# Down of a tile in parts behind up of the next, and late u and q activated by VectorE

## What is computed

```python
x_proj = silu(x @ W1 + b1);  u, v, q, k = split(x_proj, 4)       # 16 heads of 8
attn = silu(einsum('bqhd,bkhd->bhqk', qh, kh)) / S               # 16 x 2048 x 2048
av = einsum('bhqk,bkhd->bqhd', attn, vh)
y = layernorm(av * u, gamma, beta) @ W2 + b2
x = layernorm(x + y)
h = silu(fp4(x) @ fp4(w_gate).T) * (fp4(x) @ fp4(w_up).T)        # 352 wide
x = layernorm(x + fp4(h) @ fp4(w_down).T)
```

## Time and profile before

| | us |
|---|---|
| median of 3 runs | 516.2 |
| the profiled execution | 516.33 |
| its span, first to last instruction | 514.2 |
| first silu of the scores starts | 14.94 |
| last silu of the scores starts | 493.55 |
| TensorE busy | 496.7 (97%) |
| ScalarE busy | 487.3 (95%) |
| VectorE busy | 285.8 (56%) |
| POOL busy | 81.4 (16%) |
| 512 silus of the scores, busy | 474.8, mean 1182 ns for one |

### The profile page before, as it was taken

The page is one execution under the profiler, slowest core; times in us unless marked ns, Lnnn a source line. Parts: engine busy times, 40 slices in busy tenths (PEclk is TensorE's granted clock), DMA queues, the critical chain, the costliest instruction groups (busy, mean ns, idle before and its releaser), DMA issues.

```text
span 514.2 us, 20251 instructions
## 1 busy us (share of the span) xinstructions
PE 496.7 (97%) x9062; PEld 264.5 (51%) x9064; DVE 285.8 (56%) x730; ACT 487.3 (95%) x547; POOL 81.4 (16%) x180
## 2 busy tenths in 40 slices
PE   8899999999999999999999999999999999999996
PEld 5453335444344444434344444444477777777762
DVE  7644934655848375664847366573844433435445
ACT  4999999999999999999999999999999999999940
POOL 8413000102020200202020110202020202112010
PEclk9999999999999999999999999999999999999999
DMA  4732450000000000000000000000000000000000
GB/s 128 190 95 61 112 146 22 1 3 7 3 8 1 8 2 3 6 3 8 1 9 1 8 1 3 6 3 7 3 8 4 9 4 10 4 9 10 3 4 10
DMA packets 15173, 11.87 MB, mean 23 GB/s; under 512 B 1815, under 2 KB 14750, under 8 KB 15086
## 3 DMA queue, kind: packets, MB, share of 16 engines
q1 hardware_dynamic: 13800, 8.85, 6.5%
q0 software_dynamic: 704, 1.33, 0.9%
q10 hardware_dynamic: 582, 0.40, 0.3%
HBM read 1.92 MB, written 1.05 MB: 6 GB/s over the span
## 4 chain that ended last, share of the span: by engine, by line
ACT 51%; PE 28%; issue 17%; DVE 2%; DMA 1%; POOL 0%; POOLq 0%; SPq 0%; DVEq 0%
ACT attn L680 50%; PE ps L433 26%; PE ps L447 2%; DMA gate_b<-in_L_attn_b 1%; ACT feat L680 0%; ACT v_sb L680 0%; PE ps L467 0%; ACT uT L680 0%; POOL rstd_b L405 0%; DVE xn_b L817 0%; DVE stats_b L847 0%; DVE xn_b L825 0%; DVE xn_b L823 0%; DVE xn_b L821 0%; POOLq L136 0%
## 5 line engine op out<-in xcount | busy, mean ns | idle before, releaser
L680 ACT ACTIVATE attn<-ps 128x1024 f32<-128x1024 f32 x512 | 474.8, 1182 | 1.3 <-PE ps L433 0.8
L433 PE MATMUL ps<-attn,v_pad 128*32 128x256 f32 (+1 forms) x5120 | 274.4, 341 | 0.3 <-DVE wdown_t L1046 0.2
L433 PE MATMUL ps<-q_stack,k_stack 64*128 64x256 bf16 (+1 forms) x2560 | 172.9, 251 | 10.1 <-ACT attn L680 1.3
L433 PEld LDWEIGHTS ps<-attn,v_pad 128*32 128x32 f32 x5120 | 132.2, 109 | 80.3 <-issue 38.8
L433 PEld LDWEIGHTS ps<-q_stack,k_stack 64*128 64x128 bf16 x2560 | 79.0, 94 | 132.3 <-ACT attn L680 85.4
L404 POOL TENSOR_TENSOR ve_a<-mv_a,eps_col 128x1 f32<-128x1 f32 x24 | 4.6, 191 | 207.9 <-DVE mv_a L849 207.9
L404 POOL TENSOR_TENSOR ve_b<-mv_b,eps_col 128x1 f32<-128x1 f32 x24 | 4.6, 191 | 194.6 <-DVE mv_b L849 194.6
L433 PE MATMUL ps<-zeros 128*128 128x512 bf16 x49 | 13.9, 425 | 1.4 <-DVE zeros L973 1.2
L405 POOL TENSOR_TENSOR rstd_a<-ve_a,minus_half 128x1 f32<-128x1 f32 x24 | 13.5, 561 | 1.9
L405 POOL TENSOR_TENSOR rstd_b<-ve_b,minus_half 128x1 f32<-128x1 f32 x24 | 13.4, 560 | 1.9
L909 DVE COPY xqT<-ps 128x128 f32<-128x128 f32 x15 | 4.4, 292 | 16.2 <-PE ps L433 16.2
(11 more groups left out here) (189 smaller groups left out, 402.9 us busy)
## 6 DMA issues: line engine op xcount, KB each, us to landing
q_stack<-parts SPq DMA_DIRECT2D x18, 128.0 KB, 2.4
k_stack<-parts SPq DMA_DIRECT2D x12, 128.0 KB, 3.1
k_stack<-parts SPq DMA_DIRECT2D x15, 64.0 KB, 2.6
x_sb<-in_L_attn_x SPq DMA_DIRECT2D x3, 256.0 KB, 4.3
q_stack<-zeros SPq DMA_DIRECT2D x6, 128.0 KB, 2.5
k_stack<-parts POOLq DMA_DIRECT2D x9, 64.0 KB, 2.6
q_stack<-parts SPq DMA_DIRECT2D x8, 64.0 KB, 2.0
out<-x_a SPq DMA_DIRECT2D x8, 64.0 KB, 1.5
```

Source lines behind the costliest of these rows:

```text
L433: return pe.matmul(to, lhsT, rhs, start=start, stop=stop, skip_group_check=True)
L680: return act.activation(to, frm, ACT.Silu, **kw)
```

## The change

The kernel still computes the same. Three things are placed anew.

1. Down of tile t no longer is one job two steps behind its hqT. Its three products are issued behind up of tile t + 1: in three consecutive steps for wide tiles, the first two in one step and the third in the next for dense ones. up moves one step later in wide tiles. POOL makes x2 of tile t after x1 of tile t + 1.
2. u from token 512 on and q from token 1024 on are no longer projected in chunk 0. There are ten units of 256 tokens (`LATE`), one for each wide tile, projected in step +1 or +17 of the tile's chunk and activated by VectorE, in the way of `activate_gate` and in the buffers of the other tile: `late_read` at the unit's own job, `late_exponent` behind the copy of xqT, `late_sum` behind the copy of hqT, `late_product` (and a q's split) behind the next unit's `late_read`, or behind `late_sum` for the last.
3. The jobs of the weights come earlier, in steps 25, 27, 29 and 31 instead of 29, 31, 32 and 33. SP zeroes the rows of all q units first and copies the late parts in its loop over the tiles' outputs.

```diff
-               12: ("u", 0), 14: ("q", 256), 16: ("u", 1), 18: ("q", 512), 20: ("u", 2), 22: ("q", 1024),
-               24: ("u", 3), 26: ("q", 1536), 29: ("w2", 0), 31: ("gate", 0), 32: ("up", 0), 33: ("down", 0)}
+               12: ("u", 0), 14: ("q", 256), 18: ("q", 512), 25: ("w2", 0), 27: ("gate", 0), 29: ("up", 0),
+               31: ("down", 0)}
...
-    EVEN = {"y": 3, "xqT": 7, "gate": 8, "up": 10, "hqT": 16, "down": 18}
-    ODD = {"y": 19, "xqT": 23, "gate": 24, "up": 26, "hqT": 32, "down": 34}
+    EVEN = {"y": 3, "xqT": 7, "gate": 8, "up": 11, "hqT": 16}
+    ODD = {"y": 19, "xqT": 23, "gate": 24, "up": 27, "hqT": 32}
...
+    LATE = {0: ("q", 1024), 1: ("u", 512), 2: ("q", 1280), 3: ("u", 768), 4: ("q", 1536),
+            5: ("u", 1024), 6: ("q", 1792), 7: ("u", 1280), 8: ("u", 1536), 9: ("u", 1792)}
+    LW = 256
+    LATE_AT = {t: BEGIN[t // 2 + 1] + (17 if t % 2 else 1) for t in LATE}
+    PARTS_AT = {}
+    for t in range(1, DENSE + 1):
+        base, offsets = TILE_AT[t]
+        if t < WIDE:
+            first = base + offsets["up"] + 2
+            PARTS_AT |= {first: (t - 1, (0,)), first + 1: (t - 1, (1,)), first + 2: (t - 1, (2,))}
+        else:
+            first = base + offsets["up"] + 1
+            PARTS_AT |= {first: (t - 1, (0, 1)), first + 1: (t - 1, (2,))}
...
             for n in range(KT):
+                if n in LATE and LATE[n] in unit_no:
+                    stack(sp, unit_no[LATE[n]])
                 sp.wait_ge(x2_ready, n + 1)
...
+            def down_parts(at):
+                tile, parts = PARTS_AT[at]
+                k = job_no[("down", 0, tile)]
+                if at in FIRST_PARTS:
+                    wait_bank(at, k, JOB_BANK[k])
+                last = down_of(ROWS[tile % 2], JOB_BANK[k], 0, parts)
+                if at in JOB_AT:
+                    last.then_inc(job_made, 1)
...
+            def late_read(tile):
+                x, n, f, spare = late_buffers(tile)
+                col = 0 if LATE[tile][0] == "u" else 1
+                bank = wait_made("late", 0, tile)
+                dve.tensor_scalar(x, ps[:, bank, 0:LW], b1_col[:, col:col + 1], X_MIN,
+                                  ALU.add, ALU.max).then_inc(job_by_vec, 1)
+                wait_taken("late", 0, tile)
+
+            def late_exponent(tile):
+                x, n, f, spare = late_buffers(tile)
+                link(dve.tensor_scalar(n, x, -LOG2_E, Y_MIN, ALU.mult, ALU.max))
+                link(dve.tensor_scalar(spare, n, ROUND, None, ALU.add))
+                link(dve.scalar_tensor_tensor(out=f, in0=spare, scalar=ROUND, in1=n,
+                                              op0=ALU.subtract, op1=ALU.subtract))
+                link(dve.tensor_scalar(n.bitcast(U32), spare.bitcast(U32), 23, None, ALU.logical_shift_left))
+                link(dve.scalar_tensor_tensor(out=spare, in0=f, scalar=POWERS[4] / LAST, in1=f, op0=ALU.add, op1=ALU.mult))
+
+            def late_sum(tile):
+                x, n, f, spare = late_buffers(tile)
+                for power in (3, 2, 1):
+                    link(dve.scalar_tensor_tensor(out=spare, in0=spare, scalar=POWERS[power] / LAST, in1=f,
+                                                  op0=ALU.add, op1=ALU.mult))
+
+            def late_product(tile):
+                x, n, f, spare = late_buffers(tile)
+                kind, start = LATE[tile]
+                link(dve.scalar_tensor_tensor(out=spare, in0=spare, scalar=POWERS[0] / LAST, in1=n,
+                                              op0=ALU.add, op1=ALU.mult))
+                link(dve.tensor_scalar(spare, spare, LAST, 1.0, ALU.mult, ALU.add))
+                link(dve.reciprocal(f, spare))
+                link(dve.tensor_tensor(spare, x, f, ALU.mult))
+                if kind == "q":
+                    split(kind, start)
...
+                elif kind == "late":
+                    late_read(tile)
+                    if tile - 1 in LATE:
+                        late_product(tile - 1)
                 elif kind == "xqT":
                     copy_xqT(tile)
+                    if tile in LATE:
+                        late_exponent(tile)
...
                 elif kind == "hqT":
                     copy_hqT(tile)
+                    if tile in LATE:
+                        late_sum(tile)
+                        if tile + 1 not in LATE:
+                            late_product(tile)
```

More of the change, by code:

```diff
@@ L115, in build @@
         TILE_AT[t] = (BEGIN[WIDE // 2 + 1] + LAG + 1 + 12 * (t - WIDE),
-                      {"y": 0, "xqT": 4, "gate": 5, "up": 7, "hqT": 10, "down": 11})
+                      {"y": 0, "xqT": 4, "gate": 5, "up": 7, "hqT": 10})
     TILE_AT[DENSE] = (BEGIN[-2] + LAG, {"y": 1, "xqT": 5, "gate": 6, "up": 8, "hqT": 12})
+    LATE = {0: ("q", 1024), 1: ("u", 512), 2: ("q", 1280), 3: ("u", 768), 4: ("q", 1536),
[11 more added lines that the diff above has]
+            PARTS_AT |= {first: (t - 1, (0, 1)), first + 1: (t - 1, (2,))}
     JOB_AT = {at: (kind, i, None) for at, (kind, i) in PREP_AT.items()}
+    JOB_AT |= {at: ("late", 0, t) for t, at in LATE_AT.items()}
     for t, (base, offsets) in TILE_AT.items():
         JOB_AT |= {base + d: (kind, 0, t) for kind, d in offsets.items()}
+    JOB_AT |= {at: ("down", 0, t) for at, (t, parts) in PARTS_AT.items() if 2 in parts}
+    FIRST_PARTS = {at: t for at, (t, parts) in PARTS_AT.items() if 0 in parts}
     JOBS = [JOB_AT[at] for at in sorted(JOB_AT)]
@@ L318, in _ @@
                 zero_rows(sp, n)
-                stack(sp, n)
+            for start in (256, 512):
+                stack(sp, unit_no[("q", start)])
             for n in range(KT):
+                if n in LATE and LATE[n] in unit_no:
+                    stack(sp, unit_no[LATE[n]])
                 sp.wait_ge(x2_ready, n + 1)
@@ L411, in normalise, with make_x2 @@
                                           ALU.subtract, ALU.mult)
+            def make_x2(tile):
+                r = ROWS[tile % 2]
+                rstd(r, 2)
+                if tile >= 2:
+                    pool.wait_ge(out_written[tile % 2], 16 * (tile // 2))
+                normalise(r, r.x2[:, :], 2).then_inc(x2_ready, 1)
             for tile in range(TAIL - 1):
@@ L417, in _ @@
                 normalise(r, r.x1[:, :], 1).then_inc(x1_ready, 1)
[L418 to L421, removed]
+                if tile:
+                    make_x2(tile - 1)
             before = ROWS[(TAIL - 1) % 2]
@@ L562, in wait_spare, with wait_bank @@
                     pe.wait_ge(head_act, head_last[bank] + 1)
[L564 to L567, removed]
+            def wait_bank(at, k, bank):
                 if k:
@@ L574, in job @@
                     pe.wait_ge(av_taken, STEPS[at - LAG][0])
-                if tile is not None:
+            def down_parts(at):
[6 more added lines that the diff above has]
+                    last.then_inc(job_made, 1)
+            def job(at):
+                kind, i, tile = JOB_AT[at]
+                k = job_no[(kind, i, tile)]
+                bank = JOB_BANK[k]
+                wait_bank(at, k, bank)
+                if kind == "late":
+                    last = project(bank, *LATE[tile], LW)
+                elif tile is not None:
                     last = behind(kind, tile, bank)
@@ L612, in hqT_of, with down_of @@
                 return last
-            def down_of(r, small, off):
-                for t, (f0, fn) in enumerate(FT):
+            def down_of(r, small, off, parts=(0, 1, 2)):
+                for t in parts:
+                    fn = FT[t][1]
                     last = mm_rows(small, off, r.hqT[0:fn, t, :], wdown_t[0:fn, t, :], D, start=(t == 0), stop=(t == 2))
@@ L631, in behind @@
                     pe.wait_ge(hq_ready, tile + 1)
-                    return hqT_of(r, bank)
-                return down_of(r, bank, 0)
+                return hqT_of(r, bank)
             for at in range(len(STEPS)):
@@ L638, in _ @@
                     times_v(at - LAG)
[L639 removed]
+                if at in PARTS_AT:
+                    down_parts(at)
+                elif at in JOB_AT:
                     job(at)
@@ L779, in split @@
                     dve.wait_ge(head_act, head_no[(kind, start)] + 1)
-                else:
+                elif (kind, start) not in LATE.values():
                     dve.wait_ge(job_by_act, ACT_JOBS.index(job_no[(kind, start, None)]) + 1)
@@ L931, in activate_gate, with late_buffers @@
                 link(dve.reciprocal(f, spare))
+            def late_buffers(tile):
+                o = ROWS[(tile + 1) % 2]
+                kind, start = LATE[tile]
+                to = uT[:, start:start + LW] if kind == "u" else feat[:, unit_no[LATE[tile]] % FEAT, 0:LW]
+                return o.gate[:, 0:LW], o.magic[:, 0:LW], o.xn[:, 0:LW], to
+            def late_read(tile):
[20 more added lines that the diff above has]
+                x, n, f, spare = late_buffers(tile)
+                kind, start = LATE[tile]
```

(2 more changed lines are left out.)

7 lines of the change are left out of this document (4 added, 3 removed).

## The result

The changed kernel takes 518.75 us, the median of six runs (517.52 to 519.01), against 516.2: a ratio of 1.0046 with an interval of 1.0035 to 1.0057. It is slower, by 2.55 us; the forecast was 518.5. The profiled execution took 518.91 us, its span is 517.1. The times of most kernels here come in two groups up to 1.5 us apart, and in the traces this difference lies ahead of the first silu of the scores, which starts at 13.4 to 13.6 us in some and at 14.6 to 14.9 in the others. So I compare the traces from that silu on: it starts at 14.94 us before and at 14.86 after, and the last silu ends 2.93 us later behind it than before.

A forecast was written before the change was run, and what follows sets the result against it. ScalarE was taken as the bound, busy for all but half a microsecond from 80.80 to 494.90 us. Gains and losses summed to about +2.3 us on the profiled 516.33, or 518.5 from the median 516.2; range 515.4 to 520.8.

The forecast's parts named there:

- chunk 0, five activations: Chunk 0, steps 16 to 27: five 128x512 activations leave ScalarE at 0.57 us each, 2.86 us gained.
- steps 34 and 36: First chunk's end: the 0.19 us lost at step 34 goes, as the weights' gate, up and down no longer follow each other.
- dense stage, open before: Tiles 10 to 13: down and y crowding lost ScalarE 0.22 x 3 + 0.46 us; 1.1 us open to gain.
- dense stage, new: Dense tiles, steps 7 to 10: up, down's parts and hqT push TensorE's lag past 0.83; 0.13 lost five times, 0.66 us.
- four boundaries: Chunk boundaries, tiles 2, 4, 6, 8: y waits for zu behind late_product; 1.16 us lost each, 4.6 in four.
- odd tiles 1, 3, 5, 7: Product and q's split delay y and so xqT; with gate the lag is 1.05, 0.21 to 0.22 lost each, 0.84 us.
- tile 10: Step 192: late_sum and late_product of tile 9 follow hqT, so zu comes late; 0.42 us lost.
- The price of the product: late_product at 256 columns on VectorE: 3.04 us, its reciprocal 1.753 by the line through 22 and 352 columns.
- the free lag of 0.83: Score loop: TensorE may lag 0.83 us before ScalarE loses; scores must start 1.45 us before their first silu's due end.
- (a): Rival at the boundaries: product at most 2.2 us, zu reaches TensorE in time, boundary losses go; 512.8 us; chance 0.14.
- (b): Rival: VectorE's chain is 0.15 us shorter at each place, 0.3 less at each boundary; 516.4 to 517.2 us; chance 0.09.
- (c): Rival: VectorE's delays pile up; each boundary costs 1.7, each odd tile 0.5; +3.4 more, 521.9 us; chance 0.09.
- (d): Rival in chunk 0: TensorE's 512-column jobs feed ScalarE, so 2.86 us isn't gained; 521.4 us; chance 0.02.

The follow-up runs named there:

- experiment 2: Changed kernel with VectorE making zu ahead of late_product and a late q's split moved behind to_out of its tile: 511.76 us, ratio 0.9918.
- experiment 3: Changed kernel, own order, without the late silu's arithmetic (late_exponent, late_sum, four instructions of late_product); VectorE only copies the biased projection: 511.73 us, ratio 0.9924.
- Experiment 5: Changed kernel with one more 256-column tensor_tensor, its result unused, at the end of every late_product: 522.44 us, ratio 1.0126.
- experiment 1: Changed kernel with VectorE making zu of a finished chunk ahead of the odd tile's late_product: 512.14 us, ratio 0.9937.
- experiment 7: Changed kernel with down whole in its old steps and POOL's x2 in the old order, late silus kept: 545.96 us, ratio 1.0586.
- experiment 4: Kernel before the change with only down in parts at its new place and POOL's x2 a tile later, no late silus: 514.97 us, ratio 0.9984.

## Why the prediction was right

The mechanism forecast is the one that was found, and the time was right to 0.3 us. That is partly luck: two of its terms were off by 1.0 and by 0.66, in opposite directions, and the sum of the ends is 0.6 over the forecast, which the medians of the two kernels, 2.55 apart, don't show in full. In ScalarE's ends, between the kernel before and the changed one:

| term | forecast | measured |
|---|---|---|
| chunk 0, five activations | -2.86 | -2.71 |
| steps 34 and 36 | -0.19 | -0.28 |
| dense stage, open before | -1.1 | -1.13 |
| dense stage, new | +0.66 | 0 |
| four boundaries | +4.6 | +4.88 |
| odd tiles 1, 3, 5, 7 | +0.84 | +1.84 |
| tile 10 | +0.42 | +0.34 |
| sum | +2.3 | +2.94 |

The last silu of the scores ends 2.93 us later than before, each counted from its kernel's first; behind it the order is the same, and the profiled execution is 2.58 longer.

*ScalarE.* Five activations at 0.57 was the right price: experiment 2, with the same chunk 0, ends it 2.83 us earlier than before. The changed kernel's profile lost another 0.12 in step 5, which that one doesn't show. The 0.61 estimated from the Trainium skill ("ScalarE: Activation LUTs", What ACT_TABLE_LOAD costs) would have made the gain 3.07; the traces speak for 0.57. The rule of the Trainium skill ("ScalarE: Activation LUTs", Rules for kernel authors) that ScalarE is the only option for exp and the like doesn't hold in this kernel: experiments 2 and 3 show 2560 columns of silu on VectorE at no cost to the last silu's end.

*The price of the product.* The line through two reciprocals gave 1.753; the trace has 1.75. The wait for zu is 0.97 where 1.1 was forecast, and a boundary 1.22 where it was 1.16. Its three pieces can be read: hqT is 0.19 later behind the silus (0.66 against 0.47; forecast 0.2), the read of late comes 0.08 later behind hqT (2.66 against 2.58; forecast 0.09), since from the start of its projection to the read it is 0.76 (139.81 to 140.57) where the working had 0.68, and 0.06 more is in 0.15 from zu's end (144.54) to the matmul instead of 0.12 and in y's 0.58 to the next scores (144.69 to 145.27) instead of 0.55. Experiment 5 confirms that the price counts in full, experiment 1 that it goes with the order.

*Odd tiles.* Mechanism right, size off: 0.37 instead of 0.21, and 0.72 once. TensorE at tile 1:

```profile
119.00 0.90 PE L463 MATMUL ps<-q_stack,k_stack 64*128 64x256 bf16 x8
...
121.38 0.43 PE L463 MATMUL ps<-ident,xn_b 128*32 128x128 f32 x8 [0.48 <-DVE xn_b L872]
121.74 0.61 PE L463 MATMUL ps<-q_stack,k_stack 64*128 64x256 bf16 x8
...
123.88 0.61 PE L463 MATMUL ps<-q_stack,k_stack 64*128 64x256 bf16 x8
```

Scores due at 119.00+1.83 = 120.83 begin at 121.74: a lag of 0.91, where the working had 0.75. With gate it grows to 123.88-120.83-1.83 = 1.22, by 0.31 as forecast (0.30). 1.22-0.83 = 0.39, and 0.37 was lost. So the free lag of 0.83 and the rule of the deadline hold, and what failed is a sum of small terms where the loss is what sticks out above a threshold: an error of 0.16 in 0.75 is small, but it came whole on top of a loss of 0.22. I had said that 0.1 us in the product is worth 0.8 to 1 us in the sum, yet let the range's bound go by the product's price alone. The 0.72 at tile 3 (steps 88 and 89) comes with a single pause of VectorE inside a chain of linked instructions, which no other tile of this trace shows; nor does tile 3 lose more than the others in experiments 1 and 5, while such a pause stands in other places of the traces of experiments 5 and 7. So 0.35 of the +1.84 belongs to this one execution, and why VectorE paused is open:

```profile
178.55 0.18 DVE L896 BATCH_NORM_AGGREGATE mv_b<-stats_b 128x2 f32<-128x6 f32 x1 [0.43 <-issue]
```

*Dense stage.* Here a step of the working failed: up was taken to raise the lag by 0.59 in its own step, with 0.29 regained only in the next. TensorE at tile 10:

```profile
395.88 0.62 PE L463 MATMUL ps<-q_stack,k_stack 64*128 64x128 bf16 x16
...
397.33 0.78 PE L463 MATMUL ps<-wup_t,xqT 128*32 128x352 f32 x8
398.04 0.62 PE L463 MATMUL ps<-q_stack,k_stack 64*128 64x128 bf16 x16
...
400.04 0.62 PE L463 MATMUL ps<-q_stack,k_stack 64*128 64x128 bf16 x16
...
403.87 0.62 PE L463 MATMUL ps<-q_stack,k_stack 64*128 64x128 bf16 x16
```

395.88 to 398.04 is 2.16, only 0.33 over a step. TensorE, late from gate, wasn't waiting for ScalarE ahead of up, so the 0.29 that a step has to spare is used in up's own step and not lost. From 395.88 to 403.87, four steps of 1.83 and 0.66 over: it stays under 0.83, and no silu is late. (395.88 itself is on time. It comes 5.82 after the scores at 390.06, which still waited for ScalarE: three steps and 0.32, and gate's own silu takes ScalarE 0.36 in that stretch.) Experiment 4 shows the same with no late silu in the kernel.

*The rivals.* (a), the product out of the way, was false for this kernel, and its number is about what experiment 1 gives once the order makes it true: 512.8 forecast, 512.14 measured (513.31 in the profiled execution). (b), the chain shorter, is false, the pieces were longer. (c), delays piling up beyond what the sum holds, is false: hqT is late by 0.19, no more. (d), no gain in chunk 0, is false.

*Other queues.* The first part of down waits for up's bank, five times, 0.6 us on average in the waits of weight load (0.45 was forecast). POOL's x2 and the late stacks on SP made no wait ahead of y, as taken.

*What I had not asked.* The forecast priced down's move at what it gains in the wide stage, nothing. Experiment 7 shows that in the changed kernel's order of VectorE the move carries the rest of the change: without it the kernel is 30 us slower than the one before, 27 slower than the changed one. An edit that gains little alone (1.1 us, experiment 4) can be what another edit stands on; I should have asked what each half would do without the other.

## What to carry to other kernels

Work given to a half-idle engine costs first by where it stands in that engine's queue: ahead of something that the bottleneck's feeder waits for, with the slack used up, one more instruction of 0.43 us cost 0.46 to 0.47 in each of nine places; behind it, 56 us cost nothing. So list for each queue what others wait for, put that first, and fill in long work behind it. And where a loss is only what exceeds a slack, carry the errors of all small terms into the range, since they pass one to one into the loss.

## What the runs showed of the hardware

- TensorE's granted clock fell to half within or just behind idle stretches of 2.51 and 2.52 us between dense matmuls (experiment 7, four of four) and stayed there for more than 6 us twice and for little more than 3 us twice, while with 2.35 us (its tile 10), 1.75 us (its odd tiles) and 0.97 us (the changed kernel) it stayed at 1.00. Why stretches so alike kept it low for such different times is open. The Trainium skill ("TensorE: Matmul & The Clock Gate", HAM oscillation — how this bites in real kernels) says that waits between bursts of matmuls put the array back to its slow clock. The trace agrees that a wait does it; the waits in the page's example are longer than the 2.52 us here. So a wait can be worth more than itself: at the first boundary 2.52 us of idle time came with 2.7 us that the work behind it took longer (7.09 against 4.40).
- The silus' ends keep 0.917 us a silu whether they start late (1.02 long) or early (up to 1.4 or 1.5 long), in every kernel here; the starts alone can't tell a loss.
- A tensor_scalar reading PSUM with a bias pointer takes 0.48 us at 256 columns, against 0.29 for one from SBUF without a pointer.
